# A graph-attention layer on one core: the spread of the queries and the weighted sums made by one TensorE product per pair of tiles, and the spread banks taken in turn

## The reference

```python
q = (x @ Wq + bq).reshape(n_nodes, 8, 16)          # k, v alike
q_t, k_s, v_s = q[targets], k[sources], v[sources]
scores = jnp.sum(q_t * k_s, axis=-1) * scale + (edge_features @ We + be)
max_s  = jax.ops.segment_max(scores, targets, num_segments=n_nodes)
e      = jnp.exp(scores - max_s[targets])
denom  = jax.ops.segment_sum(e, targets, num_segments=n_nodes) + 1e-10
weighted = ((e / denom[targets])[:, :, None] * v_s).reshape(scores.shape[0], -1)
agg    = jax.ops.segment_sum(weighted, targets, num_segments=n_nodes)
return layernorm(x + agg @ Wo + bo)
```

## Time and profile before

| | |
|---|---|
| median of three runs | 2608.14 us (2605.48 to 2614.73) |
| the profiled execution | 2609.25 us, its span 2607.4 us |
| mean granted clock of PE | 0.65 of full speed |
| busy: PE, PEld | 1395.8 us (54%), 933.4 us (36%), 9699 rows each |
| busy: DVE, ACT | 1341.0 us (51%), 420.9 us (16%) |
| busy: POOL | 1521.0 us (58%), of it 1499.1 us in 1564 gathers |
| moved by DMA | 290.29 MB, mean 111 GB/s; 26.3% of the 16 engines' time in POOL's gathers |

### The profile page before, as it was taken

How to read it: one execution, slowest core, us unless ns; L and a number is a source line. 1 busy time by engine, 2 the same in 40 slices (tenths; PEclk the granted TensorE clock), 3 DMA queues, 4 the chain that set the end, 5 groups by cost and what they waited for, 6 DMA issues and landing times.

```text
span 2607.4 us, 30805 instructions
## 1 busy us (share of the span) xinstructions
PE 1395.8 (54%) x9699; PEld 933.4 (36%) x9699; DVE 1341.0 (51%) x3136; ACT 420.9 (16%) x1427; POOL 1521.0 (58%) x1578
## 2 busy tenths in 40 slices
PE   4145555455645464555555555546464545555557
PEld 3033333333433343333334333334343333333334
DVE  4045455554555554545555545555454545555556
ACT  0011111111111111111111111111111111111112
POOL 6735656566566566565556565656566665656540
PEclk7555666666667666666666666666566666566666
DMA  7423333333333333333333333333333333333320
GB/s 271 140 82 97 117 103 103 118 102 124 100 118 106 120 103 121 101 109 113 101 119 105 118 108 117 104 116 106 120 104 123 100 124 95 108 117 106 119 88 7
DMA packets 115466, 290.29 MB, mean 111 GB/s; under 512 B 45765, under 2 KB 53712, under 8 KB 108264
## 3 DMA queue, kind: packets, MB, share of 16 engines
q0 software_dynamic: 75072, 205.10, 26.3%
q1 hardware_dynamic: 37484, 76.52, 8.7%
q10 hardware_dynamic: 2748, 6.69, 0.7%
HBM read 276.52 MB, written 11.67 MB: 111 GB/s over the span
## 4 chain that ended last, share of the span: by engine, by line
another core or an unknown queue 37%; PE 34%; DVE 18%; issue 8%; ACT 2%; DMA 1%; SPq 0%; DVEq 0%; ACTq 0%
PE q_banks L1133 12%; PE ps_a L1170 7%; DVE prod L780 4%; DVE score L791 3%; PE ps_e L1145 2%; PE ps_t L1110 2%; PE ps_s L1191 2%; DVE wv L801 1%; PE ps_t L1116 1%; DVE run_fwd L843 1%; PE ps_a L1212 1%; PE ps_s L1197 1%; PE ps_a L1222 1%; DVE cand L837 1%
## 5 line engine op out<-in xcount | busy, mean ns | idle before, releaser
L507 POOL DMA_INDIRECT kv_buf<-kv_table,src_i x1564 | 1499.1, 959 | 1013.8 <-DVE wv L801 569.0
L1133 PE MATMUL q_banks<-q_blk,hots 64*128 64x128 f32 x3128 | 416.4, 405 | 537.3 <-issue 263.0
L1133 PEld LDWEIGHTS q_banks<-q_blk,hots 64*128 64x128 f32 x3128 | 319.4, 277 | 655.1 <-issue 635.0
L567 ACT ACTIVATE hots<-ps_t 128x512 f32<-128x512 f32 x377 | 225.1, 597 | 1972.9 <-PE ps_t L1116 960.8
L780 DVE TENSOR_TENSOR prod<-q_banks,kv_buf 128x512 f32<-128x512 f32 (+1 forms) x392 | 269.0, 686 | 410.8 <-remote 265.5
L801 DVE TENSOR_TENSOR wv<-kv_buf,ps_w 128x512 f32<-128x512 f32 (+1 forms) x392 | 265.6, 678 | 362.8 <-remote 334.8
L1170 PE MATMUL ps_a<-wv,hots 128*64 128x136 f32 x3128 | 376.5, 379 | 5.6 <-ACT wv L608 4.8
L1212 PE MATMUL ps_a<-sums_sb,carry_from 128*1 128x136 f32 x112 | 34.3, 409 | 542.2 <-DVE sums_sb L911 542.2
L791 DVE TENSOR_REDUCE score<-prod 128x32 f32<-128x512 f32 (+1 forms) x392 | 267.1, 681 | 7.9 <-issue 0.2
L1170 PEld LDWEIGHTS ps_a<-wv,hots 128*64 128x64 f32 x3128 | 239.9, 183 | 68.3 <-issue 51.2
L1212 PEld LDWEIGHTS ps_a<-sums_sb,carry_from 128*1 128x1 f32 x112 | 4.8, 81 | 564.1 <-DVE sums_sb L911 564.1
(11 more groups left out here) (141 smaller groups left out, 1337.5 us busy)
## 6 DMA issues: line engine op xcount, KB each, us to landing
edge_f<-in_edge_blk SPq DMA_DIRECT2D x55, 1024.0 KB
kv_buf<-kv_table,src_i POOLq DMA_INDIRECT x1564
kv_table<-kv_buf ACTq DMA_DIRECT2D x12, 512.0 KB, 4.4
xt_blk<-in_x_t SPq DMA_DIRECT2D x114, 32.0 KB
out<-y_out SPq DMA_DIRECT2D x114, 32.0 KB
kv_buf<-in_x_perm SPq DMA_DIRECT2D x5, 512.0 KB, 7.8
codes<-code_table SPq DMA_DIRECT2D x108, 10.5 KB
code_table<-kv_buf SPq DMA_DIRECT2D x1, 1344.0 KB
```

What stands on the lines that cost most here:

```text
L507: pool.indirect_dma_start(kv_buf[:, b % NBUF, t, :], None, kv_table, bass.IndirectOffsetOnAxis(ap=src_i[:, column:column + 1], axis=0)).th ...
L567: one = act.activation(hots[:, v % 2, :, :].rearrange("p k n -> p (k n)"), ps_t[:, :], ACT.Relu, bias=1.0)
L1133: one = pe.matmul(ps_q[j][:, k * D:(k + 1) * D], hots[own, (v - 1) % 2, 0, k * P:(k + 1) * P], q_blk[own, b % QBUF, :], start=True, stop=True)
```

## The change

The queries get 256 columns: rows 0 to 63 of `q_blk` (the first half's nodes) keep theirs in columns 0 to 127, rows 64 to 127 in columns 128 to 255, and the rest is zero, set once. One product for a pair with the whole 128-row one-hot matrix then gives the spread queries of both tiles side by side, tile after tile, in one bank. A step's spread fits into one bank, and the two banks are used in turn by steps, so a spread waits for the multiply two steps back. The multiply reads its bank in plain order. The sums of a pair become one product as well: 128 edges by 128 nodes, with the `wv` of both tiles (2 x 136 columns) as the moving side. Of the 128x272 that come out, the two diagonal blocks of 64x136 are the sums of the halves, and the two others are not used; `copy_halves` brings the two blocks to `sums_sb` with a copy each. `copy_q` becomes two copies likewise.

```diff
--- before.py
+++ after.py
@@ -124,7 +124,7 @@
         base_bc = sb("base_bc", [P, NH])
         carry_from = sb("carry_from", [P, NH])
         xt_blk = sb("xt_blk", [P, XBUF, P])
-        q_blk = sb("q_blk", [P, QBUF, D])
+        q_blk = sb("q_blk", [P, QBUF, 2 * D])
         prod = sb("prod", [P, 2, QUAD * D])
         score = sb("score", [P, 2, H, T])
         run_fwd = sb("run_fwd", [P, H * T])
@@ -211,8 +211,7 @@
 
 
         ps_t = ps("ps_t", [P, 2 * QUAD * W])
-        q_banks = ps("q_banks", [P, 2, 512])
-        ps_q = [q_banks[:, i, :] for i in range(2)]
+        ps_q = [ps(f"ps_q{i}", [P, 512]) for i in range(2)]
         ps_w, ps_e = ps("ps_w", [P, 512]), ps("ps_e", [P, 512])
         ps_a = [ps(f"ps_a{i}", [P, 512]) for i in range(2)]
         ps_s = ps("ps_s", [P, 512])
@@ -229,7 +228,10 @@
         assert 2 * NH + KV + 1 <= 512 and EPAIRS * P <= EGROUPS * 512
 
         def sums(b):
-            return ps_a[b % 2][:, 0:WV]
+            return ps_a[b % 2][:, 0:2 * WV]
+
+        def half_sums(b, j):
+            return ps_a[b % 2][j * W:(j + 1) * W, j * WV:(j + 1) * WV]
 
         def folded(b):
             return ps_a[b % 2][W:W + 1, 2 * WV:3 * WV]
@@ -584,7 +586,8 @@
                 act.wait_ge(s_newq, b + 1)
                 if b >= QBUF:
                     act.wait_ge(s_byedge, FIRST[b - QBUF + 1])
-                act.copy(q_blk[:, b % QBUF, :], new_q).then_inc(s_qcopied, 1)
+                act.copy(q_blk[0:W, b % QBUF, 0:D], new_q[0:W, :])
+                act.copy(q_blk[W:P, b % QBUF, D:2 * D], new_q[W:P, :]).then_inc(s_qcopied, 1)
 
             def exponentials(b):
                 act.wait_ge(s_shifted, b + 1)
@@ -679,6 +682,7 @@
             dve.memset(w_e2[:, :], 0.0)
             dve.memset(be_col[:, :], 0.0)
             dve.memset(eps_c[:, :], LN_EPS)
+            dve.memset(q_blk[:, :, :], 0.0)
             dve.memset(carried[:, :], 0.0)
             dve.memset(seq_left[:, 1:2], GFAR)
             dve.memset(seq_far[:, :, SEQ:SEQ + 1], FAR)
@@ -777,10 +781,9 @@
                 dve.wait_ge(s_kv[b % NBUF][g], 16 * landed)
                 if q >= 2:
                     dve.wait_ge(s_dot, q - 1)
-                dve.tensor_tensor(prod[:, q % 2, 0:n * D].rearrange("p (k j d) -> p j k d", j=2, d=D),
-                                  q_banks[:, :, 0:n // 2 * D].rearrange("p j (k d) -> p j k d", d=D),
-                                  kv_buf[:, b % NBUF, t0:t1, 0:D].rearrange("p (k j) d -> p j k d", j=2),
-                                  ALU.mult).then_inc(s_product, 1)
+                dve.tensor_tensor(prod[:, q % 2, 0:n * D].rearrange("p (t d) -> p t d", d=D),
+                                  ps_q[q % 2][:, 0:n * D].rearrange("p (t d) -> p t d", d=D),
+                                  kv_buf[:, b % NBUF, t0:t1, 0:D], ALU.mult).then_inc(s_product, 1)
 
             def dot(q):
                 b, g = STEPS[q]
@@ -904,7 +907,9 @@
                 dve.wait_ge(s_carrysum, b + 1)
                 if b >= 2:
                     dve.wait_ge(s_left, b - 1)
-                dve.tensor_copy(sums_sb[:, b % 2, :], sums(b)).then_inc(s_halves, 1)
+                for j in range(2):
+                    one = dve.tensor_copy(sums_sb[j * W:(j + 1) * W, b % 2, :], half_sums(b, j))
+                one.then_inc(s_halves, 1)
 
             def add_folded(b):
                 dve.wait_ge(s_folded, b + 1)
@@ -1124,14 +1129,11 @@
                 t0, t1 = STEP[b][g]
                 pe.wait_ge(s_qcopied, b + 1)
                 pe.wait_ge(s_copied, HOTS_TO[v - 1])
-                if q >= 1:
-                    pe.wait_ge(s_product, q)
-
-                for u in range(t1 - t0):
-                    j, k = u % 2, u // 2
-                    own = slice(j * W, (j + 1) * W)
-                    one = pe.matmul(ps_q[j][:, k * D:(k + 1) * D], hots[own, (v - 1) % 2, 0, k * P:(k + 1) * P],
-                                    q_blk[own, b % QBUF, :], start=True, stop=True)
+                if q >= 2:
+                    pe.wait_ge(s_product, q - 1)
+                for k in range((t1 - t0) // 2):
+                    one = pe.matmul(ps_q[q % 2][:, k * 2 * D:(k + 1) * 2 * D], hots[:, (v - 1) % 2, 0, k * P:(k + 1) * P],
+                                    q_blk[:, b % QBUF, :], start=True, stop=True)
                 one.then_inc(s_byedge, 1)
 
             def edge_terms(b, g):
@@ -1165,16 +1167,16 @@
                     pe.wait_ge(s_yin, b - 1)
                     pe.wait_ge(s_carried, b - 1)
 
-                for u in range(t1 - t0):
-                    own = slice(u % 2 * W, (u % 2 + 1) * W)
-                    one = pe.matmul(sums(b)[own, :], hots[:, (v - 1) % 2, 1, u * W:(u + 1) * W], wv[:, q % 2, u, :],
-                                    start=(t0 + u < 2), stop=False)
+                for k in range((t1 - t0) // 2):
+                    one = pe.matmul(sums(b), hots[:, (v - 1) % 2, 1, k * P:(k + 1) * P],
+                                    wv[:, q % 2, 2 * k:2 * k + 2, :].rearrange("p j w -> p (j w)"),
+                                    start=(t0 + k == 0), stop=False)
                 one.then_inc(s_summed, 1)
 
             def sum_carry(b):
                 if b >= 1:
                     pe.wait_ge(s_carried, b)
-                pe.matmul(sums(b), ident[0:1, :], carried[:, :], start=False, stop=True).then_inc(s_carrysum, 1)
+                pe.matmul(sums(b)[:, 0:WV], ident[0:1, :], carried[:, :], start=False, stop=True).then_inc(s_carrysum, 1)
 
             def fold_halves(b):
```

## The result

The changed kernel takes 2623.61 us in the median of 20 runs (2607.1 to 2638.8), the kernel before beside it 2610.67 us (2601.36 to 2624.11): a ratio of 1.0052, 95% interval 1.0035 to 1.0068. Measured once more beside the kernel before on another chip, it was at 1.0025 (1.0003 to 1.0048). It is slower by 0.5% (13 us) in the first measurement and 0.25% in the second, whose interval nearly reaches 1. The forecast was 2540 us, faster by 2.7%.

A forecast was written before the change was run, and what follows sets the result against it. Gathers were taken to set the pace, with POOL pausing because PE's completions stick by instruction count. 2609 - 82 (fewer pauses) + 5 (copies) + 12 - 3 (ends and start) = 2541, said as 2540 us; range 2320 to 2780.

The forecast's parts named there:

- What bounds the kernel: Steady part: gathers set the pace; PE's completions stick while gathers run, by instruction count, 1.3 us each.
- The number of pauses: POOL's waits for the weigh in the steady part: 2.54 a block in place of 3.04, saving 82 us.
- the budget of instructions: Under gather traffic PE passes 71 instructions until it sticks: 1.45 steps before, 2.16 after.
- the length of a pause: POOL's pause in the steady part, taken as 2.94 us beyond the usual 0.3, before and after.
- So as long as completions stick, this time lies inside time in which PE now stands still: Steady part: PE's longer products, +1.42 us a step or +9.9 us a block, were taken as hidden.
- The prices of the products: PE's wider products at granted clock 0.65: spreads +0.62 us and sums +0.80 us a step.
- Banks in turn: Spread waiting for the multiply two steps back: counted 0, with up to 100 us as the far end.
- The copies in two: Copies of q on ACT and half sums on DVE become two each: +5 us taken, 31 us at most.
- the ends: Stretches without gathers, 145 to 180 us and after 2537 us: +12 us; the start, 80 to 145 us: -3.
- The third: Rival for the whole kernel: fewer pauses, each ending on a longer product, 2600 to 2620 us; chance 0.08.
- The first: Rival: delay belongs to gather traffic, longer products come on top, +336 us to 2945, or 2780 or 2700; chance 0.32.
- What would show it: Signs: first multiplies about 10 us apart sooner, steady waits 137 to about 115, mean near 3.2 us, PE about 70%.

The follow-up runs named there:

- spreads_one_back: Kernel before with only the wide spreads of the change, each spread still waiting for the multiply one step back; ratio 1.0000 to the kernel before.
- spreads_alone: Kernel before with the change's wide spreads, two banks in turn and queries' columns, but the old sums; ratio 0.9895 to the kernel before.
- one_plain: Kernel before with the table of source indices loaded in the set-up by POOL instead of SP; 2050.54 us, kernel before beside it 2051.71 us.
- nogather_before: Kernel before with POOL's gathers left out from the fourth block on; 1703.21 us, kernel before beside it 2630.01 us.

## Why the prediction was wrong, step by step

- **What bounds the kernel.** The late signals were read rightly from the waits put down to "remote", and that gathers bring them was shown by leaving them out. That each late instruction costs 1.3 us at the start held too: 10 us for a spread of eight, 21.7 us for the edge products.
- **The number of pauses.** 2.54 a block were forecast instead of 3.04, from "71 instructions, pass under traffic until it sticks". It came out as 2.36 instead of 3.06, and the steps under traffic as 1.96 instead of 1.28 (2.16 instead of 1.45 were reckoned). But the budget of instructions is not borne out: with 41 or 65 instructions a step there are as many pauses as with 49, and the free start of a burst looks like a time. That the number met the forecast is in part luck.
- **The failed step is the length of a pause, held at 2.94 us**: the sum let PE get through "2.94 / 4.88 = 0.60 step in the pause" after the change, where it had 0.85, and priced the gain as 0.50 x 2.94 us. A pause does not end after a time; it ends when one step more is weighed, as the prediction itself had said, and one whole weigh ends in each, before and after. With the longer stream it lasts 4.13 us beyond the usual 0.3 instead of 2.95, and PE's records in it grew by as much, 1.34 to 2.53 us. 2.36 x 4.13 = 9.8 us a block stand against 9.0 before and 2.54 x 2.94 = 7.5 in the forecast: a gain of 1.5 us a block became a loss of 0.8 (0.4 in the repeats).
- **"So as long as completions stick, this time lies inside time in which PE now stands still"** failed with it. In the pauses PE does not stand still, and what it streams there is waited for. Counted to its signals PE was taken for 95% of the time; busy time of 54% said nothing on that.
- **The prices of the products.** +0.62 and +0.80 us were forecast, +0.40 and +0.47 measured. The shape was right: the spread takes 2.05 us at the lower level (84.95 above), where 1.96 was reckoned. What failed was to keep the clock at 0.65; it rose to 0.76, and with half of the time at the upper level a spread is 0.52 x 1.03 + 0.48 x 2.05 = 1.52 us, near the 574.6 / 392 = 1.47 of the page. Inside the pauses the clock rose little or not (0.62 before and 0.63 after; 0.63 and 0.68 in the repeats).
- **Banks in turn, at 0.** Measured 1.0%, 27 us, within the far end of 100 us that was kept. The reason given, that ACT's copy of the match is stuck behind the same signals, does not hold often enough: PE's waits for the multiply, 102.1 us in spreads_one_back, are gone in spreads_alone, and those for the copy fell from 168.1 to 7.4 us.
- **The copies in two**, +5 us, and the ends, +12 and -3, were not measured apart.
- **The rivals.** The third, that it cancels, 2600 to 2620 us, is what happened, 4 us above its end, and by its own mechanism: fewer pauses, but each ends on a longer product. It had a chance of 0.08, too little where a gain of 82 us stood against a stream of 1.42 us a step. The first had the right direction and put 336 us on a stream that cost 13 with its gain against it. The range of 2320 to 2780 held the time.
- **What would show it.** The first multiplies come at 70.70, 80.97, 94.97 and 131.37 us instead of 80.95, 105.44, 130.64 and 155.23, 10, 24, 36 and 24 us sooner. That was named as proof of the theory; it proved it for the start alone. The waits "from 137 to about 115" came out too (105 pauses), but not that "their mean stays near 3.2 us" (4.44). PE's share of the span reached 59%, not 70%.
- Beyond the sum, the whole of it rests on a condition that one plain load on POOL's queue removes. Where it is removed POOL paces both kernels alike: 2279.56 and 2282.19 us with the same breaks.

## What to carry to other kernels

Where consumers start long after a product's record has ended, count the producer as taken until its signal, and price longer products at full length in the stretches that are waited for, even if its busy share is 54%. Where a wait ends with a piece of work, its length changes with the work: ask what ends a pause before multiplying a number of pauses by a fixed length, and count pauses by their gaps, since a view's count can hold waits of 0.3 us. A mechanism measured in a pure stretch, such as the start, has a price there; take its share of the steady state from a steady stretch before multiplying. And run the kernel before beside every experiment: the largest gain here, 2617 to 2051 us by one line, showed first as a kernel before that was suddenly 21% faster.

## What the runs showed of the hardware that I had not expected

- Gathers by POOL delay PE's signals: 1.3 us for each PE instruction at the start, 1.0 product record a us late in a burst. No signal of DVE or ACT is over 0.02 us late in the same traces, as far as its event is there. Plain loads of the same bytes from SP do not; from POOL neither (1618 us), though there the remedy is in the same program.
- This goes away, in all runs of a set, when one of its programs has a plain load issued by POOL: medians of 2051 and 2052 us for the kernel before in three sets, 2611 to 2630 us in the five others, on one chip both (2630.01 and 2051.65 us).
- The Trainium skill, "NOTIFIC — the notification-queue block", section 7.1, was weighed in the prediction as a candidate for what throttles PE. one_plain leaves the same 9699 product records and as many of loads as the kernel before and has no late signal, so the number of records does not do it by itself. Semaphore events are missing where signals are late, of PE's 9 and 14% in before and after, of DVE's 32 and 30%, of ACT's 21 and 34%; in one_plain and nogather_before it is 0.5% or less of each. Whether that belongs to the cause is not shown, and the cause stays open.
- The granted clock follows the width of the products: without gathers 0.75 in the kernel before and 0.87 in the changed one, at nearly equal busy time (1082.22 and 1094.38 us). A wider product then costs less on the wall than its columns say. Why the clock is granted so is not shown.
